# First attention of a two-layer gated transformer: the high and low halves of the transposed probabilities taken two tiles at a time

## The chip, the core and the metric

The kernel runs on one core of one Trainium2 chip. The metric is the device time of one execution in microseconds (us), lower is better. The engines are PE (TensorE, with its weight loads shown apart as PEld), DVE (VectorE), ACT (ScalarE), POOL (GpSimd) and SP (SyncE); each works through its own instructions in order and waits for the others by semaphores.

## What is computed

The whole program is two layers, each a gated cross attention and a gated feed-forward part, on 4 batches of 512 tokens of width 512. The change touches the attention of the first layer alone. Cut to that, the reference is:

```python
q = _qdq(x) @ _qdq(wq).T + bq                      # 4 x 512 tokens, 16 heads of 32
kv = cond @ wkv.T + bkv
attn = softmax(einsum('bnhd,bmhd->bhnm', q, k) / sqrt(Dh), axis=-1)   # 64 maps of 512 x 512
o = einsum('bhnm,bmhd->bnhd', attn, v)
out = _qdq(o) @ _qdq(wp).T + bp
```

There are 64 (batch, head) maps of 512 x 512 probabilities. They are computed in 256 tiles of 128 query rows by 512 keys, four tiles to a head.

## The kernel before

`l0_attention` runs the 256 tiles through a software pipeline that is written out by hand for every engine. `pipeline(eng, count, unroll, stages)` makes step s of an engine call each of its stages for tile s minus that stage's lag, in the order of the list. Lags count tiles. 32 steps (two groups of four heads) are unrolled in a loop.

For one tile, the work goes round like this:

- **scores** (PE, lag 0, L874): one 128x512 product into one of three PSUM banks `pS` (`SB = 3`). It waits until the exponential that used the same bank has been read out (L873).
- **maxima** (DVE, lag 0, L952): the negated row maximum of that bank.
- **exps** (ACT, lag 1, L925): the exponential from the bank into an SBUF tile, with row sums; the trace shows it as an ACTIVATE and an ACTIVATION_READ_ACCUMULATOR.
- **transposes** (PE, lag 3, L882): four 128x128 transposes of the probabilities into one of three PSUM banks `pT` (`TB = 3`). They wait for the exponential of this tile and until `low` has left the bank.
- **high** (ACT, lag 3, L934): the bank is rounded into `PTh`, the high half.
- **low** (DVE, lag 4, L959): bank minus `PTh` into `PTl`, the low half.
- **values** (PE, lag 9, L898 and L899): two 128x512 products, of `PTh` and of `PTl`, accumulated in `pO` over the eight tiles of two heads.
- After every eighth tile (`pair_end`): **o_copy** (ACT, lag 9, L942) takes `pO` out, **o_transposes** (PE, lag 10, L910) turns it, **sum_parts** (DVE, lag 10, L970 and L972) makes the reciprocal of the row sums and adds the parts, and POOL scales them (L827).

The order on each engine follows from the lists: on PE a step is transposes, scores, values, o_transposes; on ACT it is high, exps, o_copy; on DVE it is low, maxima, sum_parts. The wait of the scores is set by `reuse(r, SB, 32)`: the number of tiles since the bank was last used. It is 3, but for the first three tiles of every 32, since 3 does not divide 32: there it is 2, 2 and 5. PSUM has eight banks, all in use: three `pS`, three `pT`, `pO`, `pR`. SP loads the operands of a group of four heads while the one before is worked on. The stage is closed by a barrier of all engines (L130) before the output stage starts.

Of the kernel before, what the change touches and what calls it, by code (L numbers as in the profile page):

```python
# [11 lines left out]
ALU = mybir.AluOpType  # L12
# [3 lines left out]
P = 128  # L16
# [11 lines left out]
def wait(eng, sem, value):  # L28

    if not (isinstance(value, int) and value <= 0):  # L30
        eng.wait_ge(sem, value)
# [8 lines left out]
def pipeline(eng, count, unroll, stages, straight_end=0):  # L40

    lag_max = max(lag for _, lag in stages)

    def step(i, u):
        for fn, lag in stages:
            q, r = divmod(u - lag, unroll)
            fn(i + q, r)

    for s in range(lag_max):
        for fn, lag in stages:
            if s >= lag:
                fn(*divmod(s - lag, unroll))
    turns = (count - lag_max - straight_end) // unroll
    if turns == 1:
        for u in range(unroll):
            step(0, lag_max + u)
    elif turns > 1:
        with eng.Fori(0, turns) as i:  # L60
            for u in range(unroll):
                step(i, lag_max + u)
    for s in range(lag_max + max(turns, 0) * unroll, count + lag_max):
        for fn, lag in stages:
            if 0 <= s - lag < count:
                fn(*divmod(s - lag, unroll))
# [137 lines left out]
HG0 = P // DH0  # L204
# [466 lines left out]
def l0_attention(nc, g, t, written, shared):  # L671
# [3 lines left out]
    QT = BT = S // P  # L675
# [1 line left out]
    PAIRS = HG0 // 2  # L677
    V_LOADS = ((0, 0, 1), (2, 1, 2), (5, 3, 1))
    NG = B * H0 // HG0
    SB, TB = 3, 3  # L680
    N = NG * UN
    with Mem(nc, "b") as m:
        O = m.sb("o", [P, 2, QT, P])
# [7 lines left out]
        PTh = m.sb("probsT_hi", [P, HG0, QT, S], F32R)  # L691
        PTl = m.sb("probsT_lo", [P, HG0, QT, S], F32R)
# [3 lines left out]
        rsum = m.sb("rowsum", [P, 2 * HG0, QT])  # L696
        rinv = m.sb("rowsum_inv", [P, 2, 2, QT])
        pS = [m.ps(f"scores{j}", [P, S]) for j in range(SB)]
        pT = [m.ps(f"pT{j}", [P, QT, P]) for j in range(TB)]
        pO = m.ps("pO", [P, S])  # L700
        pR = m.ps("pR", [P, QT, P])

# [9 lines left out]
        exp_done, hi_done, lo_done, o_mm = m.flag("exp", depth=6), m.flag("hi"), m.flag("lo", depth=6), m.flag("o_mm", depth=16)  # L712
# [71 lines left out]
        def place(r):  # L784
            return r // UN, r % UN // QT, r % QT

        def pair_end(r):

            return r % (2 * QT) == 2 * QT - 1

        def pair_buffer(r):
            return r // (2 * QT) % 2
# [71 lines left out]
        def _(pe):  # L864
# [37 lines left out]
            def o_transposes(i, r):  # L902
                if not pair_end(r):
                    return
                np = i * 2 * PAIRS + r // (2 * QT)
                pe.wait_ge(oT_done.sem, oT_done.done(np))
                pe.wait_ge(summed.sem, summed.past(np, 1))
                m.wait_apart(pe)
                for k in range(QT):
                    last = nc.tensor.transpose(pR[:, k], Os[:, pair_buffer(r), bass.ts(k, P)],  # L910
                                               g["ident"][:])
                last.then_inc(oTr_done.sem, 1)
# [3 lines left out]
        @block.scalar  # L916
        def _(act):
            def exps(i, r):
                n, np = i * 2 * UN + r, i * 2 * PAIRS + r // (2 * QT)
                gb, h, q = place(r)  # L920
                act.wait_ge(nmax_done.sem, nmax_done.done(n))
                act.wait_ge(tr_done.sem, tr_done.past(n, 4))
                if q == 0 and h % 2 == 0:
                    act.wait_ge(o_done.sem, o_done.past(np, 4))
                nc.scalar.activation(Pr[:, r % 4], pS[r % SB][:], ACT.Exp, bias=nmax[:, r % 4:r % 4 + 1],  # L925
                                     accum_out=rsum[:, gb * HG0 + h, q:q + 1]).then_inc(exp_done.sem, 1)

            def high(i, r):
                n = i * 2 * UN + r
                gb, h, q = place(r)  # L930
                act.wait_ge(tr_done.sem, tr_done.done(n))
                if q == 0:
                    wait(act, o_mm.sem, o_mm.past(n - (HG0 - 1) * QT, 1))
                nc.scalar.copy(PTh[:, h, :, bass.ts(q, P)], pT[r % TB][:]).then_inc(hi_done.sem, 1)  # L934

            def o_copy(i, r):
                if not pair_end(r):
                    return
                n, np = i * 2 * UN + r, i * 2 * PAIRS + r // (2 * QT)
                act.wait_ge(o_mm.sem, o_mm.done(n))  # L940
                act.wait_ge(oTr_done.sem, oTr_done.free(np))
                nc.scalar.copy(Os[:, pair_buffer(r)], pO[:]).then_inc(oT_done.sem, 1)  # L942

            pipeline(act, N, 2 * UN, [(high, 3), (exps, 1), (o_copy, 9)])

        @block.vector
        def _(dve):
            def maxima(i, r):
                n = i * 2 * UN + r
                dve.wait_ge(s_done.sem, s_done.done(n))  # L950
                dve.wait_ge(exp_done.sem, exp_done.past(n, 4))
                nc.vector.tensor_reduce(nmax[:, r % 4:r % 4 + 1], pS[r % SB][:], axis=AX, op=ALU.max,  # L952
                                        negate=True).then_inc(nmax_done.sem, 1)

            def low(i, r):
                n = i * 2 * UN + r
                gb, h, q = place(r)
                dve.wait_ge(hi_done.sem, hi_done.done(n))
                nc.vector.tensor_tensor(PTl[:, h, :, bass.ts(q, P)], pT[r % TB][:],  # L959
                                        PTh[:, h, :, bass.ts(q, P)], ALU.subtract).then_inc(lo_done.sem, 1)  # L960

            def sum_parts(i, r):

                if not pair_end(r):
                    return
                np = i * 2 * PAIRS + r // (2 * QT)
                gb, h, q = place(r)
                head = gb * HG0 + h - 1
                dve.wait_ge(o_done.sem, o_done.free(np))
                nc.vector.reciprocal(rinv[:, pair_buffer(r)], rsum[:, head:head + 2]).then_inc(summed.sem, 1)  # L970
                dve.wait_ge(oTr_done.sem, oTr_done.done(np))
                nc.vector.tensor_reduce(osum[:, pair_buffer(r)], pR[:].rearrange("p k (h w c) -> p k h c w", h=2, w=2),  # L972
                                        axis=AX, op=ALU.add).then_inc(summed.sem, 1)

            pipeline(dve, N, 2 * UN, [(low, 4), (maxima, 0), (sum_parts, 10)])
# [2628 lines left out]
def attend_output(nc, g, t, written):  # L3604


    with Mem(nc, "bc") as m:
        shared = AttentionOutput(m)
        l0_attention(nc, g, t, written, shared)
        l0_output(nc, g, t, shared)  # L3610
# [106 lines left out]
```

## Time and profile before

| | |
|---|---|
| median of 3 runs | 3120.47 us (3116.66 to 3122.2) |
| the profiled execution's own time | 3125.14 us |
| its span in the trace | 3123.4 us |
| granted TensorE clock, mean over the span | 0.973 of full |
| PE busy | 2916.9 us (93%) |
| DVE busy | 2315.6 us (74%) |
| ACT busy | 2083.3 us (67%) |
| POOL busy | 1416.3 us (45%) |

The first attention takes the stretch from about 169 to 523 us of the span. In a timeline row the first number is the start, the second the duration, then come engine, line, operation, what is written and what is read, and the count; a bracket tells how long the engine was idle before it and what released it. Instructions overlap at their ends, so the distance from start to start, and not the duration, is what an instruction costs an engine that never waits. A row with x4 merges four instructions and its duration runs to the end of the last.

### The profile page before, as it was taken

What the parts mean: (1) busy time and instruction counts of PE and PEld (TensorE: products, weight loads), DVE (VectorE), ACT (ScalarE), POOL (GpSimd) and SP (SyncE); (2) the same over time, 40 slices, a digit from 0 to 9 for tenths busy, and PEclk for the clock granted to TensorE, in tenths of its full rate; (3) what the DMA queues carried; (4) which work ended last, traced back from release to release, by engine and by line L of the source; (5) the groups of instructions that cost most, each with busy time, mean ns of one, the idle gap of its engine ahead of it and who ended that gap; (6) DMA issues with size and microseconds to landing.
All of it is one profiled execution on the core that took longest, in us unless ns stands there. A gap on an engine that the chain in (4) does not pass through costs nothing. (4 is left out here: it accounts for less than half of the span.)

```text
span 3123.4 us, 56345 instructions
## 1 busy us (share of the span) xinstructions
PE 2916.9 (93%) x15383; PEld 2376.0 (76%) x15414; DVE 2315.6 (74%) x4667; ACT 2083.3 (67%) x4262; POOL 1416.3 (45%) x1793
## 2 busy tenths in 40 slices
PE   6969997887999999899999899999999999899988
PEld 4657775776888877788888688888888888688755
DVE  5679998755777658767676289888998988734377
ACT  4469996422666546566666588888888888633366
POOL 3413101312001075367687377777777777442132
PEclk9989998998999999999999999999999999999999
DMA  6898663216888586545456532332322322195410
GB/s 196 271 216 197 163 171 102 78 56 234 289 258 282 170 285 208 156 143 171 142 169 186 162 96 73 99 94 76 99 91 79 99 90 80 49 322 183 163 40 34
DMA packets 401823, 474.32 MB, mean 152 GB/s; under 512 B 52276, under 2 KB 267220, under 8 KB 401652
## 3 DMA queue, kind: packets, MB, share of 16 engines
q1 hardware_dynamic: 388692, 419.72, 44.6%
q0 software_dynamic: 12960, 52.61, 5.0%
q8 instruction: 72, 1.18, 0.2%
q14 instruction: 99, 0.81, 0.1%
HBM read 304.30 MB, written 167.92 MB: 151 GB/s over the span
## 5 line engine op out<-in xcount | busy, mean ns | idle before, releaser
L2869 POOL TENSOR_SCALAR h_probs<-h_exp,h_rowsum_inv 128x512 f32<-128x512 f32 x512 | 359.0, 701 | 277.4 <-PE h_pT L2717 260.9
L2797 DVE TENSOR_REDUCE h_neg_max<-h_scores 128x1 f32<-128x512 f32 x512 | 349.3, 682 | 145.5 <-PE h_scores L2709 145.4
L2759 ACT ACTIVATE h_exp<-h_scores,h_neg_max 128x512 f32<-128x512 f32 x512 | 355.7, 695 | 110.6 <-DVE h_neg_max L2797 100.9
L2810 DVE TENSOR_TENSOR h_probsT_lo<-h_pT,h_probsT_hi 128x512 fp32r<-128x512 f32 x512 | 348.1, 680 | 0.0
L2717 PEld LDWEIGHTS h_pT<-ident,h_probs 128*128 128x128 f32 x2048 | 255.8, 141 | 71.5 <-POOL h_probs L2869 1.8
L2717 PE MATMUL h_pT<-ident,h_probs 128*128 128x128 f32 x2048 | 307.3, 272 | 0.9 <-POOL h_probs L2869 0.8
L2768 ACT CAST h_probsT_hi<-h_pT 128x512 fp32r<-128x512 f32 x512 | 301.1, 588 | 0.9 <-PE h_pT L2717 0.9
L2985 PE MATMUL k_acc<-k_w_hi,k_cat 128*128 128x512 f32 x512 | 200.9, 392 | 12.3 <-POOL k_w_lo L3066 11.4
L2732 PE MATMUL h_pO<-h_probsT_hi,n_lo 128*128 128x512 f32 x512 | 203.3, 397 | 0.0
L2986 PE MATMUL k_acc<-k_w_lo,k_cat 128*128 128x512 f32 x512 | 200.4, 391 | 0.0
L925 ACT ACTIVATE b_probs<-b_scores,b_neg_max 128x512 f32<-128x512 f32 x256 | 184.2, 719 | 14.6 <-DVE b_neg_max L952 14.6
L952 DVE TENSOR_REDUCE b_neg_max<-b_scores 128x1 f32<-128x512 f32 x256 | 173.6, 679 | 20.4 <-PE b_scores L874 20.4
L2971 ACT CAST k_cat<-k_cat 128x512 fp32r<-128x512 bf16 x128 | 79.2, 621 | 161.5 <-PE k_acc L2986 143.3
L2554 DVE TENSOR_TENSOR g_normed<-g_pQ,g_rstd 128x512 f32<-128x512 f32 x160 | 110.2, 689 | 96.1 <-PE g_pT L2458 89.6
L934 ACT CAST b_probsT_hi<-b_pT 128x512 fp32r<-128x512 f32 x256 | 156.1, 610 | 29.4 <-PE b_pT L882 29.4
L959 DVE TENSOR_TENSOR b_probsT_lo<-b_pT,b_probsT_hi 128x512 fp32r<-128x512 f32 x256 | 173.5, 678 | 0.0
L2588 POOL TENSOR_TENSOR g_rstd<-g_var_eps,neg_half 128x4 f32<-128x4 f32 x160 | 166.3, 1039 | 13.5 <-POOL g_var_eps L2586 0.2
L2856 POOL TENSOR_TENSOR n_lo<-n_raw,n_hi_second 128x512 fp32r<-128x512 f32 x128 | 165.5, 1293 | 0.0
L882 PE MATMUL b_pT<-ident,b_probs 128*128 128x128 f32 x1024 | 156.1, 275 | 3.7 <-DVE b_probsT_lo L959 2.4
L2856 POOL TENSOR_TENSOR n_lo<-n_raw,n_hi_first 128x512 fp32r<-128x512 f32 x120 | 155.3, 1294 | 0.0
L882 PEld LDWEIGHTS b_pT<-ident,b_probs 128*128 128x128 f32 x1024 | 125.8, 142 | 38.8 <-issue 8.5
L2494 ACT ACTIVATE g_squares<-g_pQ 128x512 f32<-128x512 f32 x160 | 95.4, 597 | 83.8 <-PE g_pQ L2448 77.5
(460 smaller groups left out, 9051.3 us busy)
## 6 DMA issues: line engine op xcount, KB each, us to landing
e_w_raw<-in_w SPq DMA_DIRECT2D x24, 1792.0 KB, 8.1
lnT<-g_out SPq DMA_DIRECT2D x160, 256.0 KB, 2.3
n_raw<-lnT SPq DMA_DIRECT2D x64, 512.0 KB, 5.1
e_w_raw<-in_w SPq DMA_DIRECT2D x24, 896.0 KB, 9.9
n_raw<-lnT SPq DMA_DIRECT2D x64, 256.0 KB, 5.3
n_raw<-v SPq DMA_DIRECT2D x64, 256.0 KB, 5.6
cat<-h_cat SPq DMA_DIRECT2D x128, 128.0 KB, 1.8
k_cat<-cat SPq DMA_DIRECT2D x128, 128.0 KB, 4.4
```

What stands on the lines that cost most here:

```text
L882: last = nc.tensor.transpose(pT[r % TB][:, k], Pr[:, r % 4, bass.ts(k, P)], g["ident"][:])
L925: nc.scalar.activation(Pr[:, r % 4], pS[r % SB][:], ACT.Exp, bias=nmax[:, r % 4:r % 4 + 1], accum_out=rsum[:, gb * HG0 + h, q:q + 1]).then ...
L2717: last = nc.tensor.transpose(pT[r % 4][:, k], Pn[:, r % 4, bass.ts(k, P)], g["ident"][:])
L2732: nc.tensor.matmul(pO[h][:], vl, PTh[:, br * HPG + h, k], start=False, stop=(k == QT - 1)).then_inc(o_mm.sem, 1)
L2759: nc.scalar.activation(Pr[:, r % 4], pS[r % 2][:], ACT.Exp, bias=nmax[:, r % 4:r % 4 + 1], accum_out=rsum[:, r % 4:r % 4 + 1]).then_inc(ex ...
L2768: nc.scalar.copy(PTh[:, br * HPG + h, :, bass.ts(q, P)], pT[r % 4][:]).then_inc(hi_done.sem, 1)
L2797: v.tensor_reduce(nmax[:, r % 4:r % 4 + 1], pS[r % 2][:], axis=AX, op=ALU.max, negate=True).then_inc(nmax_done.sem, 1)
L2810: v.tensor_tensor(PTl[:, br * HPG + h, :, bass.ts(q, P)], pT[r % 4][:], PTh[:, br * HPG + h, :, bass.ts(q, P)], ALU.subtract).then_inc(lo_ ...
L2856: nc.gpsimd.tensor_tensor(Lo[:, gb, slot], Raw[:, gb, slot], Hi[gb][:, slot], ALU.subtract).then_inc(op_lo.sem, 1)
L2869: nc.gpsimd.tensor_scalar(Pn[:, r % 4], Pr[:, r % 4], rinv[:, r % 4:r % 4 + 1], 1.0, ALU.mult, ALU.mult).then_inc(norm_done.sem, 1)
L2985: nc.tensor.matmul(bank[:], lhsT, Wh[:, k], start=(k == 0), stop=False)
L2986: ins = nc.tensor.matmul(bank[:], lhsT, Wl[:, k], start=False, stop=(k == CK - 1))
```

## The change

The high and low halves are taken for two tiles in one operation of 128x1024 elements: `high` and `low` return at once for an even tile, and for an odd one they handle it and the tile before it. The transposes' banks become four (`TB = 4`), allocated as two tiles of two banks each, so that one operation can read both. PSUM stays at eight banks: the scores have two (`SB = 2`). The lags and the order of the stages stay. `reuse(r, 2, 32)` is 2 for every tile, `reuse(r, 4, 32)` is 4 for every tile.

```diff
-    SB, TB = 3, 3
+    SB, TB = 2, 4
...
-        pT = [m.ps(f"pT{j}", [P, QT, P]) for j in range(TB)]
+        pTT = [m.ps(f"pT{j}", [P, 2, QT, P]) for j in range(TB // 2)]
+        pT = [pTT[j // 2][:, j % 2] for j in range(TB)]
...
+        def two_tiles(tile, h, q):
+
+            return tile[:, h, :, bass.ts(q // 2, 2 * P)].rearrange("p k (u c) -> p u k c", u=2)
...
             def high(i, r):
+
+                if r % 2 == 0:
+                    return
                 n = i * 2 * UN + r
                 gb, h, q = place(r)
                 act.wait_ge(tr_done.sem, tr_done.done(n))
-                if q == 0:
-                    wait(act, o_mm.sem, o_mm.past(n - (HG0 - 1) * QT, 1))
-                nc.scalar.copy(PTh[:, h, :, bass.ts(q, P)], pT[r % TB][:]).then_inc(hi_done.sem, 1)
+                if q == 1:
+                    wait(act, o_mm.sem, o_mm.past(n - 1 - (HG0 - 1) * QT, 1))
+                nc.scalar.copy(two_tiles(PTh, h, q), pTT[r % TB // 2][:]).then_inc(hi_done.sem, 2)
...
             def low(i, r):
+
+                if r % 2 == 0:
+                    return
                 n = i * 2 * UN + r
                 gb, h, q = place(r)
                 dve.wait_ge(hi_done.sem, hi_done.done(n))
-                nc.vector.tensor_tensor(PTl[:, h, :, bass.ts(q, P)], pT[r % TB][:],
-                                        PTh[:, h, :, bass.ts(q, P)], ALU.subtract).then_inc(lo_done.sem, 1)
+                nc.vector.tensor_tensor(two_tiles(PTl, h, q), pTT[r % TB // 2][:], two_tiles(PTh, h, q),
+                                        ALU.subtract).then_inc(lo_done.sem, 2)
```

## Rows read from the trace of the kernel before

**Rows 1.** The page, part 5: busy time and mean duration of groups of instructions.
```profile
L925 ACT ACTIVATE b_probs<-b_scores,b_neg_max 128x512 f32<-128x512 f32 x256 | 184.2, 719 | 14.6 <-DVE b_neg_max L952 14.6
L952 DVE TENSOR_REDUCE b_neg_max<-b_scores 128x1 f32<-128x512 f32 x256 | 173.6, 679 | 20.4 <-PE b_scores L874 20.4
L934 ACT CAST b_probsT_hi<-b_pT 128x512 fp32r<-128x512 f32 x256 | 156.1, 610 | 29.4 <-PE b_pT L882 29.4
L959 DVE TENSOR_TENSOR b_probsT_lo<-b_pT,b_probsT_hi 128x512 fp32r<-128x512 f32 x256 | 173.5, 678 | 0.0
```
**Rows 2.** Busy time by stretch: one full stretch of the first attention.
```profile
core 0: us, PE busy (x) PEld busy (x) DVE busy (x) ACT busy (x) POOL busy (x), PEclk, DMA share, GB/s
350.00:400.00 50.00, 46.24 (x282) 37.60 (x281) 48.22 (x85) 46.87 (x119) 3.58 (x6) 1.00 0.71 165
```
**Rows 3.** Timeline, DVE alone: four operations in a row, then a pair's end.
```profile
301.21 0.68 DVE L959 TENSOR_TENSOR b_probsT_lo<-b_pT,b_probsT_hi 128x512 fp32r<-128x512 f32 x1
301.81 0.68 DVE L952 TENSOR_REDUCE b_neg_max<-b_scores 128x1 f32<-128x512 f32 x1
302.41 0.68 DVE L959 TENSOR_TENSOR b_probsT_lo<-b_pT,b_probsT_hi 128x512 fp32r<-128x512 f32 x1
303.61 0.19 DVE L970 RECIPROCAL b_rowsum_inv<-b_rowsum 128x8 f32<-128x8 f32 x1
303.85 0.69 DVE L972 TENSOR_REDUCE b_o_sum<-b_pR 128x256 f32<-128x512 f32 x1
304.45 0.68 DVE L959 TENSOR_TENSOR b_probsT_lo<-b_pT,b_probsT_hi 128x512 fp32r<-128x512 f32 x1
```
**Rows 4.** Timeline, DVE: the sums that end pair 1 and pair 31 of 32.
```profile
197.83 0.69 DVE L972 TENSOR_REDUCE b_o_sum<-b_pR 128x256 f32<-128x512 f32 x1 [0.39 <-PE b_pR L910]
516.57 0.69 DVE L972 TENSOR_REDUCE b_o_sum<-b_pR 128x256 f32<-128x512 f32 x1 [1.30 <-PE b_pR L910]
```
**Rows 5.** Timeline, PE and ACT: scores that waited for an exponential, and what follows.
```profile
300.13 0.69 ACT L925 ACTIVATE b_probs<-b_scores,b_neg_max 128x512 f32<-128x512 f32 x1
300.72 0.20 ACT L925 ACTIVATION_READ_ACCUMULATOR b_probs<-b_scores,b_neg_max 128x1 f32 x1
300.97 0.50 PE L874 MATMUL b_scores<-b_k_stack,b_q_stack 128*128 128x512 f32 x1 [0.37 <-ACT b_probs L925]
301.31 0.40 PE L898 MATMUL b_pO<-b_probsT_hi,b_v 128*128 128x512 f32 x1
301.33 0.69 ACT L925 ACTIVATE b_probs<-b_scores,b_neg_max 128x512 f32<-128x512 f32 x1
301.77 0.60 PE L882 MATMUL b_pT<-ident,b_probs 128*128 128x128 f32 x4
```
**Rows 6.** Timeline, PE and ACT: the end of a pair of heads, from the copy on.
```profile
302.01 0.57 ACT L942 COPY b_oT<-b_pO 128x512 f32<-128x512 f32 x1
302.64 0.50 PE L898 MATMUL b_pO<-b_probsT_hi,b_v 128*128 128x512 f32 x1
303.64 0.60 PE L882 MATMUL b_pT<-ident,b_probs 128*128 128x128 f32 x4
304.28 0.59 ACT L934 CAST b_probsT_hi<-b_pT 128x512 fp32r<-128x512 f32 x1 [0.53 <-PE b_pT L882]
304.76 0.69 ACT L925 ACTIVATE b_probs<-b_scores,b_neg_max 128x512 f32<-128x512 f32 x1
305.34 0.20 ACT L925 ACTIVATION_READ_ACCUMULATOR b_probs<-b_scores,b_neg_max 128x1 f32 x1
```
**Rows 7.** Groups of instructions by shape, of ACT and DVE: 1024 elements, and 512 of the same kind.
```profile
L392 ACT CAST a_wkv_hi<-a_wkv_raw 128x1024 fp32r<-128x1024 f32 x4 | 4.2, 1045 | 4.4 <-DMA a_wkv_raw<-in_wkv0T 4.4
L388 ACT CAST a_ctx_hi<-a_ctxT 128x512 fp32r<-128x512 f32 x16 | 9.8, 611 | 3.6 <-DMA a_ctxT<-in_ctxT 3.6
L477 DVE TENSOR_TENSOR a_wkv_lo<-a_wkv_raw,a_wkv_hi 128x1024 fp32r<-128x1024 f32 x4 | 4.9, 1225 | 13.9 <-ACT a_wkv_hi L392 13.7
```
**Rows 8.** Timeline at half clock: the fifth scores and what follows them.
```profile
179.50 0.80 PE L874 MATMUL b_scores<-b_k_stack,b_q_stack 128*128 128x512 f32 x1 [5.68 <-DMA b_k_stack<-qk]
180.09 1.05 PE L882 MATMUL b_pT<-ident,b_probs 128*128 128x128 f32 x4
181.18 0.59 ACT L934 CAST b_probsT_hi<-b_pT 128x512 fp32r<-128x512 f32 x1 [6.07 <-PE b_pT L882]
```
**Rows 9.** Busy time by stretch, columns as in rows 2: PE four fifths busy, two cases.
```profile
570.00:590.00 20.00, 16.32 (x104) 13.00 (x104) 13.74 (x27) 9.60 (x19) 5.15 (x11) 1.00 0.17 54
1220.00:1240.00 20.00, 16.06 (x65) 12.79 (x64) 14.83 (x18) 9.58 (x15) 3.62 (x5) 0.85 0.46 137
```

## Prediction

> **What bounds the stage now.** I read the page first, for the four operations of the change and their neighbours [rows 1]. DVE takes a maximum (679 ns) and a low half (678 ns) for every tile, ACT an exponential (719 ns) and a high half (610 ns). The busy time by stretch then shows who has room in the first attention [rows 2]: of 50 us DVE is busy 48.22, ACT 46.87, PE 46.24, at full clock. So DVE is the bound, and the other two are close behind. The DVE timeline shows how it is full [rows 3]: one operation starts every 0.60 us, with no idle time between, although each lasts 0.68. Eight tiles are 16 such operations, 9.6 us, and a pair of heads ends with a reciprocal (0.24 from start to start) and a sum (0.60): 10.4 us in all. The real distance between pair ends is (516.57 - 197.83) / 30 = 10.62 us [rows 4], so some 0.2 us of eight tiles is waiting. The stage ends in a barrier, so what it loses or gains goes fully into the kernel's time.
>
> **What the wider operations save.** On DVE 128 low halves of 1024 elements take the place of 256 of 512. A subtraction of 1024 elements lasts 1225 ns elsewhere in this kernel [rows 7]; less the 0.08 by which operations overlap it costs 1.145 us, against 2 x 0.60 for two: 0.05 saved, 0.2 in eight tiles, 6 us over the 128. On ACT a cast of 1024 elements lasts 1045 ns where one of 512 lasts 611 [rows 7]: the second half costs 0.43 more, against 0.48 for a separate cast (start to start, the cast at 304.28 and the exponential at 304.76) [rows 6]. These rows read SBUF and the new operations read PSUM, so the saving on DVE may lie between nothing (two full costs) and 0.13 (512 more elements took 1225 - 678 = 547 ns, and 678 - 547 = 131 ns is all that one operation has beside its elements); I take 0.05. None of it matters if DVE is no longer what the stage waits for.
>
> The Trainium skill, Perfetto Trace Analysis, section Optimizing Scalar/DVE Operations, says that both engines pay a fixed access cost for each instruction (about 125 ns for DVE on PSUM), and that grouping into larger operations helps if the engine is saturated. DVE is saturated here [rows 2], and 128 instructions fewer would be 16 us by the page's figure. The next section of mine is why I don't follow it; it is the first rival.
>
> **What the two score banks cost.** Scores of tile n now wait for the exponential of tile n - 2, not n - 3. Lay out two tiles, with an even step 2p. ACT does high(2p-4, 2p-3), exp(2p-1), exp(2p). PE does in step 2p+1: transposes(2p-2), scores(2p+1), values(2p-8); and in step 2p+2: transposes(2p-1), scores(2p+2), values(2p-7). ACT's next operation is high(2p-2, 2p-1), which needs transposes(2p-1). These stand on PE behind scores(2p+1), which wait for exp(2p-1), which on ACT stands behind the high before. This closes a ring: high, exp(2p-1), scores(2p+1), values(2p-8), transposes(2p-1), high. It is gone round once for two tiles. Its legs:
> - high start to the end of the next exponential's accumulator read: 304.28 to 305.34 + 0.20 = 305.54, so 1.26 us [rows 6]; with 512 elements more, 1.26 + 0.43 = 1.69.
> - From there to the scores' start: 300.92 to 300.97, 0.05; scores to values 0.34 (300.97 to 301.31); values, both products, to transposes 0.46 (301.31 to 301.77) [rows 5]. The score wait in that group is one of the few at distance 2 in the kernel before, so it is the leg itself that is seen.
> - Transposes start to the high that waited for them: 303.64 to 304.28, 0.64 [rows 6]; I take 0.65.
>
> Sum: 1.69 + 0.05 + 0.34 + 0.46 + 0.65 = 3.19 us for two tiles. Today they take 10.62 / 4 = 2.66. In the kernel before the ring is open: the transposes of a tile stand behind scores that wait for an exponential three tiles back, and the round of about 2.75 us (1.26 + 0.05 + 0.34 + 0.46 + 0.65) is spread over three tiles of 1.33.
>
> Nothing else is late inside the 3.19. From the high's start at 0: the low starts at 1.05 and frees DVE at 2.2; scores(2p+1) start at 1.74 and their maximum is ready by 3.0, while exp(2p+1) is only reached at 3.19 + 0.91 = 4.1. DVE needs 1.15 + 2 x 0.60 = 2.35, ACT 0.91 + 2 x 0.68 = 2.27 (0.68 from exponential to next operation, 301.33 to 302.01 [rows 5, 6]). The lows free the four transpose banks in time: transposes(2p) start at about 3.6 and need a low that ends at 2.3.
>
> **The pair's end.** Once in eight tiles the copy of `pO` comes between exp(2p-1) and exp(2p), and values(2p-8) need it. From the high: 0.91 to the exponential, 0.68 to the copy, then the chain of rows 6: copy to values 0.63, values to the next tile's transposes, with the o transposes between, 1.00 (302.64 to 303.64), transposes to high 0.64. Sum 3.86 instead of 3.19: the copy costs 0.67 more. Eight tiles: 3 x 3.19 + 3.86 = 13.43 us, against 10.62: 2.81 more.
>
> **The sum.** Thirty periods: 30 x 2.81 = 84 us. Before the first pair's end the first four tiles are hidden, since the fifth scores wait for their operands until 179.50 in any case [rows 8]; from there to the sum at 197.83 [rows 4] there are 13 steps, 18.3 us, and they become 13 x 3.19 / 2 + 0.67 = 21.4: 3 us. After the last scores there is no score wait, so the tail gives back about 1. In all +86 us. The profiled execution's own time is 3125.14, so it would be 3211; it lies 4.7 us above the median of the runs. On the median, 3120.47 + 86 = 3206.5, I say 3207.
>
> What else is edited costs nothing: even tiles issue nothing, the wait of the high on `o_mm` is for products done five steps earlier, and SP, POOL and the zero stores have the same work, with more time for it.
>
> **Bounds.** The 1024 cast: 0.40 (below the 0.43 of rows 7) to 0.48 (a full second cast) [rows 6]. Transposes to high 0.60 (their own duration) to 0.67. Issue gaps of PE 0.05 each way. The ring then is 3.08 to 3.32, eight tiles 13.0 to 14.0, and the whole +72 to +108: 3192 to 3228.
>
> **Rivals.** (1) The grouping rule wins. DVE stays the bound, because the ring closes earlier than I think; that needs a round below about 2.5 us, so 0.7 less than my legs, for instance if the high did not stand between two exponentials. Then eight tiles cost 10.6 - 0.2 and the time is 3120 - 6 = 3114. For it: DVE's rows without a gap. Against: each leg is measured in the very waits it is made of. 3 in 100. (2) The ring is just as long as today's period (2.66), and nothing moves: 3120. It needs scores and values out of the ring (0.80), which the order on PE forbids. 3 in 100. (3) PE idles about a fifth of each round (from about 1.06 to 1.74 of 3.19), and the granted clock falls in part of the stage. At half clock, from scores to transposes is 0.59 and from transposes to high 1.09 [rows 8]; with values doubled to 0.92 (my estimate from full clock) the ring is 1.74 + 0.59 + 0.92 + 1.09 = 4.34, 1.15 more. If all of the stage ran so, some 128 x 1.15 and 32 pair ends at 1.3 more: +190, 3397; if a fifth did, +38, 3245. For it: a stretch with PE 80% busy had 0.85. Against: another with 82% had 1.00 [rows 9], and what precedes a low clock in the first attention itself is a wait of 5.68 us for a transfer [rows 8], eight times my gap. 9 in 100, nearly all of it for a part of the stage.
>
> The Trainium skill, TensorE: Matmul & The Clock Gate, section A second HAM failure mode: psum-queue depth-cycling, tells of a kernel whose short idle times between groups of matmuls, while it cycled through PSUM banks, made the clock swing between its two levels. No row here shows that for waits as short as these, so it sets no term.
>
> **How the numbers follow.** The ring as laid out has 85 in 100: 3207. The range takes its bounds, reaches above to a fifth of the stage at half clock and below a little for a leg that overlaps more than I see: 3182 to 3245. Faster by over 0.2% is rival 1, 0.03; within 0.2%, about what a measurement of this kernel can tell, is rival 2, 0.03; slower is the rest, 0.94.
>
> **What the profile after would show.** The stage reaches to about 610 us. DVE's busy share in it falls from 96% to about 80%. On every second scores (L874) PE waits some 0.7 us for ACT (L925), some 85 us in all where the kernel before has few; high (L934) waits some 0.8 us for PE's transposes, 128 times. The high lasts about 1.03 us, the low about 1.22. Distances between sums (L972) are 13.4 us. I am wrong if lows follow maxima without idle time, if the high's waits are gone, or if the clock is at 0.5 in stretches of the stage.

## The result, and the profile after

The changed kernel takes 3220.64 us (median; 3217.14 to 3223.74), the kernel before beside it 3120.06. The ratio is 1.0324, with a 95% interval of 1.0311 to 1.0338: 3.2% slower, about 100 us. The profiled executions are 3125.14 us before and 3219.67 after, 94.5 apart.

First the busy time by stretch, with the columns of rows 2:

```profile
200.00:250.00 50.00, 39.17 (x220) 29.61 (x218) 40.07 (x51) 36.21 (x78) 14.58 (x21) 1.00 0.77 185
...
350.00:400.00 50.00, 39.34 (x219) 29.88 (x218) 40.30 (x52) 36.79 (x78) 5.46 (x8) 1.00 0.55 133
...
550.00:600.00 50.00, 39.68 (x221) 30.24 (x222) 40.29 (x52) 35.92 (x79) 3.58 (x6) 1.00 0.32 81
```

In [rows 2] DVE was busy 48.22 of 50 us; now it is 40.30, and PE and ACT fell with it. No engine is the bound any more. The granted clock is 1.00 in every one of the eight stretches from 200 to 600 us. The stage now ends with the sum at 616.35 us.

The waits of the changed kernel between 200 and 500 us (who waited for whom, us in total, times, longest) say what is late:

```profile
PE b_scores L879 <- ACT b_probs L930: 61.4, 88, 0.7
ACT b_probsT_hi L942 <- PE b_pT L887: 44.9, 44, 1.3
ACT b_probsT_hi L942 <- issue: 38.1, 44, 0.9
DVE b_neg_max L960 <- PE b_scores L879: 29.2, 66, 0.5
DVE b_probsT_lo L970 <- ACT b_probsT_hi L942: 21.2, 88, 0.2
```

88 pairs of tiles fall into this stretch, and in each PE waits once for an exponential (L930), ACT once ahead of a high half (L942), and DVE once for that high half. PE and ACT wait for each other in turn, which is what a ring looks like in this view.

The timeline shows one round of it, from one high half to the next. Only the rows of the ring are shown; what the engines do beside it is left out, here and in the timelines below (lines of the changed kernel: high L942, exponential L930, scores L879, values L903 and L904, transposes L887):

```profile
353.49 1.01 ACT L942 CAST b_probsT_hi<-b_pT 128x1024 fp32r<-128x1024 f32 x1 [0.86 <-issue]
354.40 0.69 ACT L930 ACTIVATE b_probs<-b_scores,b_neg_max 128x512 f32<-128x512 f32 x1
354.98 0.20 ACT L930 ACTIVATION_READ_ACCUMULATOR b_probs<-b_scores,b_neg_max 128x1 f32 x1
355.24 0.50 PE L879 MATMUL b_scores<-b_k_stack,b_q_stack 128*128 128x512 f32 x1 [0.69 <-ACT b_probs L930]
355.57 0.39 PE L903 MATMUL b_pO<-b_probsT_hi,b_v 128*128 128x512 f32 x1
356.03 0.60 PE L887 MATMUL b_pT<-ident,b_probs 128*128 128x128 f32 x4
356.72 1.01 ACT L942 CAST b_probsT_hi<-b_pT 128x1024 fp32r<-128x1024 f32 x1 [0.87 <-PE b_pT L887]
```

353.49 to 356.72 is 3.23 us for two tiles. The legs: 0.91 from the high to the exponential, then 0.78 to the end of the accumulator read, 0.06 to the scores, 0.33 to the values, 0.46 to the transposes, 0.69 to the next high. The two operations that the change made wide are as long as forecast (a row each of the groups of instructions: 1014 ns for the cast, 1225 ns for the subtraction):

```profile
L970 DVE TENSOR_TENSOR b_probsT_lo<-b_pT,b_probsT_hi 128x1024 fp32r<-128x1024 f32 x128 | 156.8, 1225 | 32.3 <-ACT b_probsT_hi L942 32.2
L942 ACT CAST b_probsT_hi<-b_pT 128x1024 fp32r<-128x1024 f32 x128 | 129.7, 1014 | 120.2 <-PE b_pT L887 65.4 <-issue 54.8
```

ACT sat idle 120 us ahead of its 128 casts. In [rows 1] it was 29.4 us ahead of 256.

### The profile page after: what moved, and what is told of

Same layout as the page of the kernel before. It is cut to its first block and busy times, and to the rows that moved or that the text cites. A ratio compares the mean times of both kernels' runs of the same rounds, so it can differ in the third digit from the quotient of the medians.

```text
span 3217.7 us, 56253 instructions
## 1 busy us (share of the span) xinstructions
PE 2943.9 (91%) x15383; PEld 2380.5 (74%) x15414; DVE 2336.6 (73%) x4539; ACT 2082.5 (65%) x4134; POOL 1413.2 (44%) x1793
## 3 DMA queue, kind: packets, MB, share of 16 engines
q8 instruction: 72, 1.18, 0.2%
## 5 line engine op out<-in xcount | busy, mean ns | idle before, releaser
L879 PE MATMUL b_scores<-b_k_stack,b_q_stack 128*128 128x512 f32 x256 | 126.7, 496 | 109.5 <-ACT b_probs L930 89.3
L942 ACT CAST b_probsT_hi<-b_pT 128x1024 fp32r<-128x1024 f32 x128 | 129.7, 1014 | 120.2 <-PE b_pT L887 65.4
L930 ACT ACTIVATE b_probs<-b_scores,b_neg_max 128x512 f32<-128x512 f32 x256 | 175.4, 692 | 21.0 <-DVE b_neg_max L960 21.0
L832 POOL TENSOR_TENSOR b_o<-b_o_sum,b_rowsum_inv 128x256 f32<-128x256 f32 x32 | 20.1, 627 | 375.4 <-DVE b_o_sum L983 375.4
L970 DVE TENSOR_TENSOR b_probsT_lo<-b_pT,b_probsT_hi 128x1024 fp32r<-128x1024 f32 x128 | 156.8, 1225 | 32.3 <-ACT b_probsT_hi L942 32.2
L2599 POOL TENSOR_TENSOR g_rstd<-g_var_eps,neg_half 128x4 f32<-128x4 f32 x160 | 165.6, 1035 | 13.4 <-POOL g_var_eps L2597 0.2
L887 PE MATMUL b_pT<-ident,b_probs 128*128 128x128 f32 x1024 | 155.4, 275 | 0.0
```

## Experiments

All runs below are timed against the kernel before on the same chip, and the ratio is what compares them. "Eight tiles" is the distance between the sums of pair 1 and pair 31 on DVE, divided by 30, as in [rows 4]: 10.62 us before, (609.91 - 198.85) / 30 = 13.70 in the changed kernel.

**1. Two score banks, everything else one tile at a time.**

Against the changed kernel, `high` and `low` are again as in the kernel before:

```diff
-                if r % 2 == 0:
-                    return
...
-                nc.scalar.copy(two_tiles(PTh, h, q), pTT[r % TB // 2][:]).then_inc(hi_done.sem, 2)
+                nc.scalar.copy(PTh[:, h, :, bass.ts(q, P)], pT[r % TB][:]).then_inc(hi_done.sem, 1)
...
```

> The changed kernel's banks (two for the scores, four for the transposes), but high and low halves again for one tile at a time. Ring theory: the ring of waits (high, exponential of the tile two on, scores, values, transposes, high) stays, one cast of 512 elements shorter, 0.48 + 0.78 + 0.05 + 0.34 + 0.46 + 0.67 = 2.78 us for two tiles in place of 3.22, and the pair's end still adds 0.7: eight tiles 11.8 us, against 10.62 in the kernel before and 13.70 in the changed one, so about 3120 + 37 = 3157. Rival A (the pairing alone costs, the third score bank is worth nothing): 3120. Rival B (the third bank alone costs, whatever the width of the operations): 3221.

Measured: 1.0102 (1.0079 to 1.0125), eight tiles 11.80 us. The third score bank alone costs a third of the loss. (This run keeps the fourth transposes' bank too; no run with two score banks and narrow operations was made without it.) The timeline has the shorter ring: from one high to the second after it 2.75 us (349.99 to 352.74).

```profile
349.99 0.59 ACT L939 CAST b_probsT_hi<-b_pT 128x512 fp32r<-128x512 f32 x1 [0.70 <-PE b_pT L887]
350.47 0.69 ACT L930 ACTIVATE b_probs<-b_scores,b_neg_max 128x512 f32<-128x512 f32 x1
351.30 0.50 PE L879 MATMUL b_scores<-b_k_stack,b_q_stack 128*128 128x512 f32 x1 [0.23 <-ACT b_probs L930]
351.64 0.40 PE L903 MATMUL b_pO<-b_probsT_hi,b_v 128*128 128x512 f32 x1
352.10 0.60 PE L887 MATMUL b_pT<-ident,b_probs 128*128 128x128 f32 x4
352.74 0.59 ACT L939 CAST b_probsT_hi<-b_pT 128x512 fp32r<-128x512 f32 x1 [0.33 <-PE b_pT L887]
```

Both rivals, that the width alone or the bank alone is all of the loss, fall.

**2 and 3. Only one of the two operations wide.** In the first the high is for one tile and the low for two; in the second the other way round. The edits are those of run 1 in `high` alone and in `low` alone.

> The changed kernel with the high halves for one tile each and the low halves for two. Ring theory: the low half is no part of the ring, the high half is, so the time is that of the run with both single, about 3157, and PE's wait for ACT ahead of the scores shrinks alike. Rival C (the wide low, 1225 ns on DVE, holds back the next maximum or the transposes' banks and is what the changed kernel loses by): near 3221, with the loss staying although the high is single.

Measured: 1.011 (1.0081 to 1.0139), eight tiles 11.80 us: the same as run 1.

> The changed kernel with the high halves for two tiles and the low halves for one each. Ring theory: nothing in the ring is touched, 3.22 us for two tiles and 13.7 for eight, 3221, although DVE has 128 operations more. Rival C (the wide low is the loss): 3160 or less.

Measured: 1.0325 (1.0293 to 1.0356), eight tiles 13.70 us: the same as the changed kernel. So with two score banks and this order on PE, all that the width costs in a period comes through ACT's cast; it makes no difference whether the subtraction on DVE is wide.

**4. The values taken out of the ring.**

```diff
-            pipeline(pe, N, 2 * UN, [(transposes, 3), (scores, 0), (values, 9), (o_transposes, 10)])
+            pipeline(pe, N, 2 * UN, [(transposes, 3), (values, 9), (scores, 0), (o_transposes, 10)])
```

> The changed kernel with PE's order within a step changed from transposes, scores, values to transposes, values, scores. Ring theory: the two products of the values (0.46) leave the ring, since PE does them while it would wait for the exponential; 3.22 becomes 2.76 for two tiles. At a pair's end the values wait for the copy and then scores, o transposes and transposes follow: about 4.2 instead of 3.92. Eight tiles 3 x 2.76 + 4.2 = 12.5 us against 13.70, so 3221 - 31 x 1.2 = 3184. Rival D (what holds the ring is not PE's order but the exponential and the maximum of the bank: scores, maximum, exponential, scores): 3221 within 5.

Measured: 1.0197 (1.0171 to 1.0223), eight tiles 12.52 us. Rounds are 2.76 and 2.77 us (349.93, 352.69, 355.46), 0.46 less than 3.23, the length of the leg that was taken out:

```profile
349.93 1.01 ACT L942 CAST b_probsT_hi<-b_pT 128x1024 fp32r<-128x1024 f32 x1 [1.29 <-PE b_pT L887]
351.67 0.50 PE L879 MATMUL b_scores<-b_k_stack,b_q_stack 128*128 128x512 f32 x1 [0.25 <-ACT b_probs L930]
352.01 0.60 PE L887 MATMUL b_pT<-ident,b_probs 128*128 128x128 f32 x4
352.69 1.01 ACT L942 CAST b_probsT_hi<-b_pT 128x1024 fp32r<-128x1024 f32 x1 [0.40 <-issue]
...
355.46 1.01 ACT L942 CAST b_probsT_hi<-b_pT 128x1024 fp32r<-128x1024 f32 x1 [0.41 <-PE b_pT L887]
```

This is the plainest evidence for the ring: no bank and no operation is changed, only the order on PE.

**5. Transposes ahead of the scores.**

```diff
-            pipeline(pe, N, 2 * UN, [(transposes, 3), (scores, 0), (values, 9), (o_transposes, 10)])
+            pipeline(pe, N, 2 * UN, [(transposes, 2), (scores, 0), (values, 9), (o_transposes, 10)])
```

> The changed kernel, nothing left out, with the transposes on PE at lag 2 instead of 3, so that transposes(2p-1) stand ahead of scores(2p+1) and not behind them and the values. Ring theory: scores and values leave the ring, 1.69 + 0.05 + 0.67 = 2.41 us; the next ring, over the score, its maximum and the second exponential, is about 2.6 to 2.9 for two tiles, so eight tiles are 10.7 to 12 us and the time 3125 to 3165. Rival D (the two banks bound the round by scores, maximum and exponential alone): 3221 within 5.

Measured: 1.0112 (1.0085 to 1.0138), eight tiles 11.67 us. The old ring is open, and the next one has a different wide operation in it. In the timeline, low half (L970), transposes that wait for it, scores, maximum, next low half: 357.01 to 359.87, 2.86 us for two tiles.

```profile
357.01 1.21 DVE L970 TENSOR_TENSOR b_probsT_lo<-b_pT,b_probsT_hi 128x1024 fp32r<-128x1024 f32 x1
358.37 0.63 PE L887 MATMUL b_pT<-ident,b_probs 128*128 128x128 f32 x4 [0.20 <-DVE b_probsT_lo L970]
358.75 0.48 PE L879 MATMUL b_scores<-b_k_stack,b_q_stack 128*128 128x512 f32 x1
359.26 0.69 DVE L960 TENSOR_REDUCE b_neg_max<-b_scores 128x1 f32<-128x512 f32 x1 [0.45 <-PE b_scores L879]
359.87 1.21 DVE L970 TENSOR_TENSOR b_probsT_lo<-b_pT,b_probsT_hi 128x1024 fp32r<-128x1024 f32 x1
```

The length was forecast, the members were not: I had put the second exponential there, and not the low. That the low is a member is read from these waits; no run made it narrow in this order.

**6 to 9. The third bank given back.** To have a ninth bank, these four leave out the transposes of the outputs (`o_transposes` only passes its signal on, and `sum_parts` reads `Os` in SBUF), so `pR` is gone. The outputs of these four are thus not turned, and they are compared with one another.

> The kernel before with the transposes of the outputs left out (four 128x128 at each pair's end): the sum reads the copy in SBUF instead, so the outputs of the attention are not turned, and the PSUM bank pR is free and unused. It is the control for the next two. All theories: DVE stays the bound, 10.4 us for eight tiles, and the pair's end loses some of its 0.2 us of waiting: 0 to 7 us faster than the kernel before, 3113 to 3120.

Measured: 0.9962 (0.9947 to 0.9977), eight tiles 10.46 us. By the ratio that is 12 us less than the kernel before, where 0 to 7 were expected. One of the 30 periods takes 13.51 us, since its scores wait for the transfer of their operands; the mean of the other 29 is 10.35.

```profile
236.72 0.50 PE L873 MATMUL b_scores<-b_k_stack,b_q_stack 128*128 128x512 f32 x1 [2.92 <-DMA b_k_stack<-qk]
```

> The changed kernel with the same transposes of the outputs left out, scores still in two banks. All theories: 0.43 us less in each pair's end, 31 x 0.43 = 13 us less than the changed kernel: 3208.

Measured: 1.0268 (1.0241 to 1.0296), eight tiles 13.40 us, 0.30 less than the changed kernel where 0.43 was expected.

> As the one with two score banks and without the transposes of the outputs, but the bank that is now free is the third bank of the scores; the halves are taken for two tiles and the transposes have four banks. Ring theory: with a score wait three tiles back the scores leave the ring, which is 1.69 + 0.05 + 0.67 = 2.41 us for two tiles; DVE with 1.145 + 2 x 0.60 = 2.35 is again about as long, and eight tiles are 10.2 to 10.5 us: 3105 to 3115, up to 8 us faster than the control of the kernel before without these transposes, and some 100 faster than the run with two banks. Rival E (the wide operations by themselves are too coarse for the pipeline, whatever the banks): 3160 or more.

Measured: 1.0054 (1.0038 to 1.007), eight tiles 11.23 us. The third bank brings 13.40 - 11.23 = 2.17 us in eight tiles, 65 us in 30 periods. But this run is not faster than its control, as I had expected; it is slower by 0.9%. Rounds within a pair are 2.48 us (350.17 to 352.65), near the 2.41 that the ring was said to have without the scores. The pair's end is 3.54 us (352.65 to 356.19), and there the expectation had left out the copy. 3 x 2.48 + 3.54 = 10.98 us is what every second period takes; the others take 11.3 and 11.8 in turn, and why was not tested.

```profile
350.17 1.01 ACT L938 CAST b_probsT_hi<-b_pT 128x1024 fp32r<-128x1024 f32 x1
...
352.65 1.01 ACT L938 CAST b_probsT_hi<-b_pT 128x1024 fp32r<-128x1024 f32 x1
353.56 0.69 ACT L926 ACTIVATE b_probs<-b_scores,b_neg_max 128x512 f32<-128x512 f32 x1
...
354.23 0.59 ACT L946 COPY b_oT<-b_pO 128x512 f32<-128x512 f32 x1
...
354.87 0.50 PE L902 MATMUL b_pO<-b_probsT_hi,b_v 128*128 128x512 f32 x1
...
355.47 0.63 PE L886 MATMUL b_pT<-ident,b_probs 128*128 128x128 f32 x4
...
356.19 1.02 ACT L938 CAST b_probsT_hi<-b_pT 128x1024 fp32r<-128x1024 f32 x1 [0.69 <-PE b_pT L886]
```

The control had three transposes' banks and not four, so one more run has the same banks and differs in the width alone:

> As the run with pairs, three score banks and no transposes of the outputs, but with high and low halves for one tile each; it has the same banks, three for the scores and four for the transposes, so it differs from that run in the width of the operations alone. If the wide high is what costs 27 us there (at a pair's end it is behind the copy: high, exponential, copy, values, transposes, high, 3.54 us where other rounds take 2.48), this run is at the time of the control with three and three banks, 0.996 of the kernel before, 10.3 to 10.6 us for eight tiles. If the fourth transposes' bank or the changed bank order costs, it is near 1.005.

Measured: 0.995 (0.9933 to 0.9967), eight tiles 10.23 us. The width alone, with three score banks and four for the transposes, costs 0.99 us in eight tiles (11.226 - 10.234), some 1% of the kernel's time. Both operations differ between these two runs, so they don't tell the cast from the subtraction. In the narrow run DVE is full, as the busy time of 200 to 500 us shows (PE, PEld, DVE, ACT, POOL):

```profile
200.00:500.00 300.00, 277.98 (x1645) 222.34 (x1643) 299.87 (x527) 289.10 (x733) 55.47 (x75) 1.00 0.75 177
```

In the wide one it is not, though it has fewer operations to do in each tile (the same 300 us, as a sum of three stretches):

```profile
sum 300.00, PE 273.24 PEld 196.42 DVE 279.35 ACT 265.43 POOL 52.53; mean PE 91.08 PEld 65.47 DVE 93.11 ACT 88.48 POOL 17.51
```

**10 to 12. Can two banks be had for nothing?**

The first edit is made in the kernel of run 2, the second in that of run 2 and in the kernel before:

```diff
-            pipeline(pe, N, 2 * UN, [(transposes, 3), (scores, 0), (values, 9), (o_transposes, 10)])
+            pipeline(pe, N, 2 * UN, [(transposes, 3), (values, 9), (scores, 0), (o_transposes, 10)])
...
-            pipeline(pe, N, 2 * UN, [(transposes, 3), (scores, 0), (values, 9), (o_transposes, 10)])
+            pipeline(pe, N, 2 * UN, [(scores, 0), (transposes, 2), (values, 9), (o_transposes, 10)])
```

> Nothing left out. Two score banks, four transpose banks, high halves for one tile, low halves for two, and PE's order transposes, values, scores. Ring theory: by the run with high single the ring is 2.78 us for two tiles, and without the values' two products 2.32, which is less than DVE needs (1.145 + 2 x 0.60 = 2.35). Then DVE is the bound again, with 10.2 us for eight tiles in place of 10.4, but the pair's end still goes through the copy: 10.3 to 10.9, so 3110 to 3130. If the theory is wrong about what the second ring leg is worth, the time stays at the 3155 of the run with high single.

Measured: 1.0079 (1.0066 to 1.0092), eight tiles 11.38 us, against 11.80 in run 2 and 10.3 to 10.9 expected. Rounds within a pair are short (2.33 us from one low half, at 346.62, to the next, at 348.95), but at its end the values wait for the copy ahead of the scores, and both the scores and the maximum of DVE are late:

```profile
354.13 0.58 ACT L947 COPY b_oT<-b_pO 128x512 f32<-128x512 f32 x1
...
354.76 0.50 PE L903 MATMUL b_pO<-b_probsT_hi,b_v 128*128 128x512 f32 x1 [1.03 <-ACT b_oT L947]
...
355.32 0.39 PE L879 MATMUL b_scores<-b_k_stack,b_q_stack 128*128 128x512 f32 x1
...
355.75 0.69 DVE L957 TENSOR_REDUCE b_neg_max<-b_scores 128x1 f32<-128x512 f32 x1 [0.61 <-PE b_scores L879]
```

> Nothing left out. As the last one in banks and halves, but PE's order is scores, transposes at lag 2, values at lag 9, so that scores and transposes both come at once when their exponential is done. Ring theory: two rings are left, scores to maximum to exponential (0.78 + 0.05 + 0.53 + 0.73 = 2.09 for two tiles) and exponential to scores to transposes to high (1.8 of 2.4), both under DVE's 2.35: 10.2 to 10.6 us for eight tiles, 3107 to 3120. Rival: the wide low ahead of the odd maximum makes the ring of the maximum late by its length, as the run with transposes at lag 2 showed (2.86 for two tiles): 3150 to 3165.

Measured: 1.0019 (1.001 to 1.0029), eight tiles 10.78 us, where 10.2 to 10.6 were expected. With two score banks and 128 wide subtractions the order scores, transposes, values gives back nearly all of the loss of run 2, and still does not pay.

> The kernel before, with three banks each and all halves for one tile, and only PE's order changed to scores, transposes at lag 2, values. It parts what the order gives from what the banks and the wide low give. DVE needs 10.4 of today's 10.62 us for eight tiles, so at best 7 us: 3113 to 3122.

Measured: 1.0025 (1.0015 to 1.0035), eight tiles 10.93 us, outside what I expected (10.62 at most). One period of 12.36 us holds a wait of 1.55 us for operands and makes 0.06 of the mean. The rest of the difference is idle time of DVE, most of it ahead of the sum of a pair, which waits for the transposes of the outputs: in four periods in a row DVE is idle 0.34, 0.45, 1.01 and 0.24 us, against 0, 0.23, 0 and 0.72 in the kernel before. So this order by itself is slightly worse than the one that the kernel before has, and none of the three kernels beats it.

## Why the prediction was right

**What the two banks cost** was the step that carried the sum, and it held leg by leg. It said 3.19 us for two tiles; 3.23 was measured, the difference being 0.69 instead of 0.65 from transposes to high. Run 4 took one leg out and the round lost just that leg, run 1 shortened one leg, run 2 and run 3 showed which of the wide operations is a member.

**The pair's end** was put at 3.86 and is 3.92 (359.95 to 363.87 in the timeline after). Eight tiles should be 3 x 3.23 + 3.92 = 13.61, and every second pair has just that. The others have 13.77, since on PE another 0.2 lies between the copy and the values (347.71 to 348.55, against 361.53 to 362.17):

```profile
347.71 0.59 ACT L950 COPY b_oT<-b_pO 128x512 f32<-128x512 f32 x1
...
348.55 0.47 PE L903 MATMUL b_pO<-b_probsT_hi,b_v 128*128 128x512 f32 x1 [0.17 <-issue]
...
361.53 0.59 ACT L950 COPY b_oT<-b_pO 128x512 f32<-128x512 f32 x1
...
362.17 0.50 PE L903 MATMUL b_pO<-b_probsT_hi,b_v 128*128 128x512 f32 x1
```

By the code, these are the values that open a group of four heads and have two more waits to issue. I take these to be the cause; no run tested it.

**The sum**, in the profiled executions: 30 periods cost 30 x (13.70 - 10.62) = 92 us where 84 was said. The first pair, from the fifth scores on (176.71), takes 22.1 us instead of 18.3, 3.8 where 3 was said. The tail was mis-signed: I had it give back 1 us and it costs 1 more (from the 31st sum to the last 6.44 us, against 5.48). In this order on PE it goes with the wide high: with that alone the tail is 6.42 us, with a wide low alone 5.97, with neither 5.48 (runs 3, 2 and 1). Together +97. Against that, the fifth scores have their operands 2.8 us earlier in this execution (176.71 against 179.50). Behind the stage the two differ by 0.2, which gives the 94.5 between the profiled executions. The medians differ by 100.6, since the profiled execution before was 5 us above the median of its runs and the one after 1 us below. So the forecast of +86 was short by 8 us in the periods and by 3 in start and tail; the remaining 3 or 4 are what single executions differ by.

**What the wider operations save** was right in size (1225 ns for the low, 1014 for the high, against 1225 and 1.03 us) and right in being worth nothing here. A wide low costs 1.14 us where the next operation follows at once (611.52 to 612.66, in the changed kernel), against 2 x 0.60. But the prediction gave the width too little blame: it laid the loss on the score bank, though its own longest leg had the wide cast in it. The runs split it. With single operations the bank costs 1.18 us in eight tiles (run 1), with three banks the width costs 0.99 (runs 8 and 9), and both together 3.08. Together they cost more than their sum: one bank less lets the ring span two tiles in place of three, the wide cast makes the ring longer, and a ring costs time only as far as it is longer than DVE's work for the tiles that it spans (2.6 us for two).

**Rivals.** The first, that grouping wins, fell, and more clearly than I had argued: even with the third bank given back the wide operations lose 1%. The Trainium skill, Perfetto Trace Analysis, section Optimizing Scalar/DVE Operations, says that grouping helps where the engine is saturated. DVE was saturated here and the subtractions did get cheaper for it, yet the time rose. They got cheaper by 0.06 us a pair, less than half of the 0.125 us of that page from which the estimate of 16 us was worked out. The same section says that shorter instructions can let work complete sooner where ScalarE or VectorE is not saturated but makes bubbles on other engines. The runs agree: DVE had no room left (299.87 of 300 us in run 9), ACT had a little (289.10), and it was ACT's cast that had to stay short, which runs 2 and 3 show for two score banks. The second, a ring just as long as the old period, fell with the measured 3.23. The third, the clock, fell too: 1.00 in all stretches from 200 to 600 us, with PE waiting 0.7 us in every 3.2. The Trainium skill, TensorE: Matmul & The Clock Gate, section A second HAM failure mode: psum-queue depth-cycling, tells of short idle times that made the clock swing; in this trace waits of 0.7 us did not. One reading of mine was off there: the wait of 5.68 us for a transfer [rows 8] does not precede the low clock, it falls inside it. The granted clock of the kernel before is 0.50 from 160 to 180 us, and what comes ahead of its first scores at 169.03 is 14.75 us without work for PE. The sum of the upper bounds, redone, is some +104 and not +108; the top of the range is set by the clock rival and does not change.

What the profile was to show came out: the end of the stage (610 said, 616 measured), DVE's share (80%), PE's wait of 0.7 us ahead of every second scores (85 us in all said, 89.3 measured), the high's wait (0.8 said, 0.86 measured) and the distance of the sums (13.4 said, 13.70 measured).

## What to carry to other kernels

Before two operations are merged or a buffer is given up, write down for each engine the order of its queue and follow the waits until they close: a wide operation is paid once by its own engine, and a second time by everything that stands behind it in a ring. The length of a ring divided by the number of tiles it spans is to be compared with the busiest engine's time for a tile; a buffer less shortens the span, a wider operation lengthens the round, and the two compound. An order in which the product that nobody waits for fills the waiting time is worth trying first, since it costs no memory; look then at what happens once in a while (here the copy at a pair's end), which can eat the gain.

## What the runs showed that I had not expected

The kernel before has its waiting in one place. Its periods are 10.4, 10.6 and, one in four (one to a loop of 32 tiles), 11.1 us, and all that they are longer than 10.4 is idle time of DVE ahead of the sum of a pair, which waits for the transposes of the outputs:

```profile
314.97 0.69 DVE L972 TENSOR_REDUCE b_o_sum<-b_pR 128x256 f32<-128x512 f32 x1 [0.76 <-PE b_pR L910]
```

It is tempting to lay the 11.1 on the seam of the loop, where by the code a bank of three comes round after two tiles and not three. But run 6 has the same banks and the same seam, without the transposes of the outputs, and apart from the period that waited for operands and the one after it (11.08) its longest is 10.69. So the seam by itself doesn't cost the 0.7; what makes these transposes late in that one period stays open. With four transposes' banks (run 9) nearly all periods are 10.23 to 10.29.

ACT's operations overlap their neighbours, so a cast of 1024 elements reading PSUM (1014 ns) saves only some 0.05 us against two of 512 (610 ns each in [rows 1]): 0.91 us from its start to the next operation (353.49 to 354.40), against 2 x 0.48 (349.99 to 350.47 in run 1).
